# Second cross-attention of a two-layer decoder: scores one slot earlier, two row buffers, copies dealt out in turn

## The chip, the cores and the metric

The kernel runs on one core of a Trainium2 chip. The metric is the device time of one execution in microseconds. Five engines work side by side, each on its own in-order list of instructions, and wait for each other through counting semaphores: TensorE (PE; its weight loads are shown as PEld), VectorE (DVE), ScalarE (ACT), GpSimd (POOL) and SyncE (SP), which here only issues transfers.

## The reference

Two decoder layers over x of shape (8 batches, 256 rows, 256 features), each layer with a mixing step, a cross-attention to a context of the same shape, and a feed-forward step, each followed by residual and layer norm. The change lies in the second layer's cross-attention, 16 heads of 16 features:

```python
def _mha(key, value, query, mask, Wk, bk, Wq, bq, Wv, bv, Wo, bo):
    k, q, v = (heads(a @ W.T + b) for a, W, b in ...)      # (8, 16, 256, 16)
    scores = jnp.einsum('bhmd,bhnd->bhmn', q, k)
    scores = jnp.where(mask, scores, jnp.float32(-10000000000.0))
    attn = jax.nn.softmax(scores / jnp.sqrt(jnp.float32(DK)), axis=3)
    out = jnp.einsum('bhmn,bhnv->bhmv', attn, v)
    out = out.transpose(0, 2, 1, 3).reshape(bs, n_q, EDIM)
    return out @ Wo.T + bo
x = _layernorm(x + _L1_xattn_ref(ctx_1024, ctx_1024, x, mask, ...))
```

(the first line stands for the three projections of the reference.) The layer norm follows in the same stage, and the gated feed-forward step after it.

## The kernel before, in words

The stage is `attention_mask`, with one function per engine: `mask_pe`, `mask_act`, `mask_dve`, `mask_pool`, `mask_sp`. Every engine's list is written out by hand; nothing is reordered. Work goes in 32 rounds n = 4b + j (batch b = 0..7, j = 0..3), four heads g = 0..3 a round. For round n:

- **scores(n)** on PE (16 matmuls, L1553 in batch 0, L1556 in the others) fills four PSUM banks, one per head g. It waits until all peaks of round n-1 have read them.
- **peaks(n, g)** on DVE (L1877, two instructions a head) adds the mask bias, writes the rows to SBUF (`Sx` for g 0 and 1, `Pr` for g 2 and 3) and takes the row maximum into `mq`.
- **exps(n, g)** on ACT (L1779, two instructions a head) applies exp to the rows in place.
- **turn(n, g)** on PE (L1572, four transposes) turns the rows into one of two PSUM banks, `t_bank[g % 2]`. Heads 0 and 2 share one bank, 1 and 3 the other, so turn(n, 2) waits until head 0 has been copied out, and turn(n, 3) until head 1 has.
- **turned(n, g)** copies the bank to SBUF: DVE for g 0 and 1 (L1885), ACT for g 2 and 3 (L1787).
- **weigh(n)** on PE (16 matmuls, L1587) multiplies with the values; **copy_ot(n)** on ACT (L1796) keeps the result. weigh(n-1) is issued at the end of round n.

Because there is one set of row buffers and one `mq`, peaks(n+1, g) waits for turn(n, g). The first cross-attention of the kernel (lines 701 to 1047) does the same arithmetic with two row buffers and another order of its lists.

Once a batch, one bank `m_bank` carries in turn: the query projection of a later batch (`x1_project_q`, L242), two turnings back of the attention output (`turn_back`, L1596) with DVE's division by the row sums (`normalise`, L1895 and L1901), the transposes of it (L234) with ACT's copy (`turn_at`, L1807), the output projection (`project_rows`, L250) with DVE's residual sum and moments (`norm_begin`, parts 0, 1, 2, L201 to L216), and the transposes of the finished rows (L234) with ACT's copy (`turn_x`, L1801). POOL builds the mask bias, splits queries and keys into two parts, and finishes the layer norm; SP loads values and masks and moves the split parts between partitions.

Before the change round n on PE is: turn 0, turn 1, scores(n+1), turn 2, turn 3, then weigh(n-1); the work on `m_bank` lies between these, mostly ahead of weigh. After the 32nd round begins the gated feed-forward step: `gate_up`, `tanh`, `hidden` and so on, whose first parts are already mixed into the last round.

Of the kernel before, what the change touches and what calls it, by code (L numbers as in the profile page):

```python
# [27 lines left out]
P = 128  # L28
# [68 lines left out]
def decoder_kernel(nc, xT, ctxT, fside, mask0, mask1, wmats, cols_d, rows_d, gb, gate_up, down,  # L97
                   ident_d, rel_k_d, rel_v_d, mix_d, consts_d, out):
    ctx = ExitStack()
    with ctx:  # L100
# [1354 lines left out]
        def attention_mask(sa_y_mm, sa_y_steps, sa_biased, sa_kept, sa_xt_mm, sa_xt_sb, sa_r_out):  # L1455
# [55 lines left out]
            def down_bank(t, tt):  # L1511

                if t < B - 2:
# [8 lines left out]
            rows_of = [Sx[:, :, :, :].rearrange("p a t k -> p (a t) k"),  # L1522
                       Pr[:, :, :, :].rearrange("p a t k -> p (a t) k")]
# [11 lines left out]
            def rows_of(g, t):  # L1535

                return (Sx if g < 2 else Pr)[:, g % 2, t, 0:S]
# [23 lines left out]
            def mask_pe(pe):  # L1561

                def turn(n, g):

                    pe.wait_ge(p_exp, 4 * n + g + 1)
                    if g < 2:
                        ge(pe, pt_act, 2 * (n - 1) + g + 1)
                    else:
                        pe.wait_ge(pt_dve, 2 * n + g - 1)
                    for t in range(TT):  # L1570
                        for k in range(TT):
                            last = pe.transpose(t_bank[g % 2][:, k * S + t * P:k * S + (t + 1) * P],  # L1572
                                                rows_of(g, t)[:, k * P:(k + 1) * P], ident[:, :])
                    last.then_inc(t_mm, 1)
# [74 lines left out]

                def second_round(b, n):  # L1650

                    turn(n, 0)
                    if b >= 2:
                        pe.wait_ge(y_steps, 4 * (b - 2) + 1)
                    if b >= 3:
                        pe.wait_ge(kept, b - 2)
                        transpose_tiles(pe, m_bank, x_tok[:, b - 3, :, :], xt_mm)
                    turn(n, 1)
                    scores(pe, n + 1)
# [6 lines left out]
                    if b >= 1:  # L1666
                        if b >= 3:
                            pe.wait_ge(xt_sb, b - 2)
                        if b == 1:
                            pe.wait_ge(q_sb, 3)  # L1670
                        pe.wait_ge(ot_sb, NQ * b)
                        turn_back(b - 1, 0)
                    weigh(n - 1)

                def third_round(b, n):

                    turn(n, 0)
                    if b >= 1:
                        pe.wait_ge(normed, TT * (b - 1) + 1)
                        turn_back(b - 1, 1)  # L1680
                    turn(n, 1)
                    scores(pe, n + 1)
                    if b >= 1:
                        pe.wait_ge(normed, TT * b)
                        transpose_tiles(pe, m_bank, at, at_mm)
                    turn(n, 2)
                    turn(n, 3)
                    if b < B - 2:
                        if b >= 1:
                            pe.wait_ge(at_sb, b)  # L1690
                        else:
                            pe.wait_ge(sa_xt_sb, B)
                        x1_project_q(pe, b + 2, m_bank)
                    weigh(n - 1)
# [4 lines left out]
                def fourth_round(b, n):  # L1699

                    turn(n, 0)
                    turn(n, 1)
                    if b < B - 1:
                        scores(pe, n + 1)
                    else:
# [3 lines left out]
                    if 1 <= b < B - 1:  # L1709
                        pe.wait_ge(at_sb, b)  # L1710
                        if b < B - 2:
                            pe.wait_ge(q_sb, b + 3)
                        project_rows(pe, m_bank, aT, wo, y_mm)
# [59 lines left out]
            def mask_act(act):  # L1773

                def exps(n, g):

                    for t in range(TT):
                        act.wait_ge(s_max, TT * (4 * n + g) + t + 1)
                        last = act.activation(rows_of(g, t), rows_of(g, t), ACT.Exp,  # L1779
                                              bias=mq[:, g, t:t + 1], scale=-1.0)  # L1780
# [28 lines left out]

                for b in range(B):  # L1810
                    for j in range(NQ):
                        n = NQ * b + j
                        if n >= 1:
                            turned(n - 1, 2)
                        exps(n, 0)
                        exps(n, 1)
                        if n == 0:
                            x1_copy_q(act, 1, o_bank)
# [4 lines left out]
                        if j == 3 and b < B - 2:  # L1823
                            x1_copy_q(act, b + 2, m_bank)
                        if n >= 1:
                            turned(n - 1, 3)
                        exps(n, 2)
                        exps(n, 3)
                        if j == 1 and b >= 3:
                            turn_x(b - 3)  # L1830
                        if n >= 2:
                            copy_ot(n - 2)
                        if j == 2 and b >= 1:
                            turn_at(b - 1)

# [13 lines left out]
                turned(NQ * B - 1, 2)  # L1849
                turned(NQ * B - 1, 3)  # L1850
# [15 lines left out]
            def mask_dve(dve):  # L1866

                def peaks(n, g):
# [6 lines left out]
                    ge(dve, t_mm, 4 * (n - 1) + g + 1)  # L1875
                    for t in range(TT):
                        dve.tensor_tensor_reduce(  # L1877
                            out=rows_of(g, t), in0=s_bank[g][:, t * S:(t + 1) * S],
                            in1=x1_bias_two[:, b % 2, t, :], scale=-1.0, scalar=3e38, op0=ALU.add,
                            op1=ALU.min, accum_out=mq[:, g, t:t + 1]).then_inc(s_max, 1)  # L1880
# [25 lines left out]

                for b in range(B):
                    for j in range(NQ):
                        n = NQ * b + j
                        peaks(n, 0)  # L1910
                        peaks(n, 1)
                        if j == 2 and b >= 1:
                            normalise(b - 1, 0)
                        peaks(n, 2)
                        peaks(n, 3)
# [1456 lines left out]
```

## Time and profile before

| what | value |
|---|---|
| median of 3 runs | 820.91 us (820.75 to 822.95) |
| the profiled execution's own time | 820.36 us |
| its span in the trace | 818.6 us |
| PE busy | 778.7 us, 95% |
| DVE busy | 646.8 us, 79% |
| ACT busy | 615.9 us, 75% |
| POOL busy | 429.8 us, 53% |
| mean granted TensorE clock | 0.998 of full speed |

The 1.8 us between the execution's time and the span lie outside the trace. Busy time is shown per engine; a busy PE can still run its blocks with gaps between them that its pipelined records cover, so block starts say more than busy time. The stage of the change goes from about 561 us to about 737 us of the span.

### The profile page before, as it was taken

How to read it: one execution, taken by the hardware profiler on the slowest of the kernel's cores; microseconds unless marked ns; L12 is line 12 of the kernel's file. 1: busy time of each engine (PE TensorE's matmuls, PEld its weight loads, DVE VectorE, ACT ScalarE, POOL GpSimd, SP SyncE). 2: the span in 40 equal slices, each digit the busy share in tenths (PEclk: the TensorE clock that was granted, in tenths of full speed). 3: DMA queues.
4: the chain of work that ended last, by engine and by line, in shares of the span. 5: the costliest groups of instructions: out<-in, count | busy, mean ns of one | idle time of the engine just before them, and what ended most of it. 6: DMA issues, size and time to landing. Idle time of an engine off the chain costs nothing.

```text
span 818.6 us, 20952 instructions
## 1 busy us (share of the span) xinstructions
PE 778.7 (95%) x6901; PEld 596.0 (73%) x6901; DVE 646.8 (79%) x2457; ACT 615.9 (75%) x1602; POOL 429.8 (53%) x462
## 2 busy tenths in 40 slices
PE   9998999999999988999999999999899999999996
PEld 7876777777667766677777777777577777676785
DVE  4997888888998866778778667775888888976776
ACT  4547998888993467888887888875999999984331
POOL 0265475676755165354553644126855666335764
PEclk9999999999999999999999999999999999999999
DMA  9400663222203378988988989864121222200001
GB/s 316 153 26 35 199 188 68 79 85 86 73 15 132 127 219 278 293 256 255 283 240 255 272 242 275 268 184 158 50 65 67 68 70 69 66 2 0 27 26 53
DMA packets 105393, 115.05 MB, mean 141 GB/s; under 512 B 29061, under 2 KB 94085, under 8 KB 105030
## 3 DMA queue, kind: packets, MB, share of 16 engines
q1 hardware_dynamic: 104724, 113.35, 44.4%
q8 instruction: 57, 0.93, 0.5%
q14 instruction: 50, 0.41, 0.2%
q10 hardware_dynamic: 562, 0.35, 0.1%
HBM read 48.09 MB, written 51.82 MB: 122 GB/s over the span
## 4 chain that ended last, share of the span: by engine, by line
PE 49%; ACT 7%; DVE 5%; issue 2%; DMA 2%; POOL 1%; SPq 0%; DVEq 0%; ACTq 0%
PE bank L1572 7%; PE bank L242 6%; PE bank L2336 6%; PE bank L250 5%; PE bank L2322 3%; PE bank L2353 3%; PE bank L1587 3%; PE bank L1623 3%; PE bank L1613 3%; PE bank L1556 2%; PE bank L2388 2%; ACT Sx L1779 2%; PE bank L2370 1%; PE bank L234 1%; ACT q_heads L1787 1%
## 5 line engine op out<-in xcount | busy, mean ns | idle before, releaser
L242 PE MATMUL bank<-x_feat,w_all_mats 128*128 128x256 f32 x384 | 93.0, 386 | 1.9 <-ACT q_full L358 0.6
L242 PEld LDWEIGHTS bank<-x_feat,w_all_mats 128*128 128x128 f32 x384 | 70.4, 191 | 14.7 <-ACT rw L2711 3.8
L2669 ACT ACTIVATE bias_area<-bias_area,mq_two 128x256 f32<-128x256 f32 x128 | 66.5, 533 | 0.0
L3065 POOL TENSOR_TENSOR bnd<-bnd,consts 128x60 f32<-128x60 f32 x64 | 18.6, 312 | 81.3 <-DMA bnd<-band_scratch 81.2
L3054 POOL COPY rw<-rw 128x856 f32<-128x856 f32 x32 | 29.2, 913 | 57.9 <-ACT rw L2711 57.9
L894 ACT ACTIVATE dist<-dist,mq_two 128x256 f32<-128x256 f32 x128 | 56.0, 501 | 3.6 <-DVE mq_two L1008 3.6
L2845 DVE COPY q_heads<-bank 128x512 f32<-128x512 f32 x64 | 41.7, 685 | 21.0 <-PE bank L2336 21.0
L1779 ACT ACTIVATE Sx<-Sx,mq 128x256 f32<-128x256 f32 x128 | 54.3, 501 | 2.3 <-DVE mq L1877 2.3
L1885 DVE COPY q_heads<-bank 128x512 f32<-128x512 f32 x64 | 42.0, 684 | 17.0 <-PE bank L1572 17.0
L1008 DVE CUSTOM_DVE_ANT_0 dist<-bank,bias_area 128x256 f32<-128x256 f32 x128 | 46.5, 419 | 10.7 <-PE bank L701 5.6
L1779 ACT ACTIVATE Pr<-Pr,mq 128x256 f32<-128x256 f32 x128 | 54.5, 505 | 0.0
L1877 DVE CUSTOM_DVE_ANT_0 Sx<-bank,bias_area 128x256 f32<-128x256 f32 x128 | 46.5, 419 | 1.6 <-PE bank L1553 1.2
L2837 DVE CUSTOM_DVE_ANT_0 bias_area<-bank,dist 128x256 f32<-128x256 f32 x128 | 46.1, 420 | 1.2 <-DMA dist<-skew_scratch 1.2
L1877 DVE CUSTOM_DVE_ANT_0 Pr<-bank,bias_area 128x256 f32<-128x256 f32 x128 | 46.5, 420 | 0.0
L1787 ACT ACTIVATE q_heads<-bank 128x512 f32<-128x512 f32 x64 | 37.7, 591 | 11.5 <-PE bank L1572 11.5
L250 PE MATMUL bank<-w_all_mats,aT 128*128 128x256 f32 x192 | 46.3, 384 | 0.0
L1016 DVE COPY q_heads<-bank 128x512 f32<-128x512 f32 x64 | 43.9, 686 | 2.1 <-PE bank L713 1.9
L902 ACT ACTIVATE q_heads<-bank 128x512 f32<-128x512 f32 x64 | 38.0, 593 | 10.0 <-PE bank L713 8.9
L1572 PE MATMUL bank<-ident,Sx 128*128 128x128 f32 x256 | 38.9, 282 | 5.5 <-ACT q_heads L1787 5.1
L1572 PEld LDWEIGHTS bank<-ident,Sx 128*128 128x128 f32 x256 | 27.3, 141 | 22.1 <-issue 10.3
L2678 ACT ACTIVATE q_heads<-bank 128x512 f32<-128x512 f32 x64 | 37.8, 592 | 4.5 <-PE bank L2336 4.5
L2336 PE MATMUL bank<-ident,bias_area 128*128 128x128 f32 x256 | 39.8, 290 | 0.7 <-DVE q_heads L2845 0.6
(322 smaller groups left out, 2377.5 us busy)
## 6 DMA issues: line engine op xcount, KB each, us to landing
dist<-skew_scratch SPq DMA_DIRECT2D x64, 296.0 KB, 4.1
skew_scratch<-rw SPq DMA_DIRECT2D x30, 588.0 KB, 5.3
bnd<-band_scratch SPq DMA_DIRECT2D x64, 108.0 KB, 2.9
band_scratch<-bias_area SPq DMA_DIRECT2D x32, 162.0 KB, 3.2
band_scratch<-bias_area SPq DMA_DIRECT2D x32, 148.0 KB, 2.6
skew_scratch<-dist SPq DMA_DIRECT2D x4, 1024.0 KB, 9.1
context_values<-dist SPq DMA_DIRECT2D x8, 512.0 KB, 2.6
v_two<-context_values SPq DMA_DIRECT2D x8, 512.0 KB, 4.2
```

The lines of the kernel that those rows point to most:

```text
L242: last = pe.matmul(dst[:, m * S:(m + 1) * S], w[:, k, m * P:(m + 1) * P], rhs[:, k, :], start=(k == 0), stop=(k == FT - 1))
L250: last = pe.matmul(dst[:, t * D:(t + 1) * D], src[:, k, t * P:(t + 1) * P], w[:, k, :], start=(k == 0), stop=(k == FT - 1))
L894: last = act.activation(rows_of(n, g, t), rows_of(n, g, t), ACT.Exp, bias=mq_two[:, n % 2, g, t:t + 1], scale=-1.0)
L1008: dve.tensor_tensor_reduce(out=rows_of(n, g, t), in0=s_bank[g][:, t * S:(t + 1) * S], in1=bias_two[:, b % 2, t, :], scale=-1.0, scalar=3e3 ...
L1016: dve.tensor_copy(PTq[:, 4 * (n % 2) + g, :, :], t_bank[g % 2][:, :].rearrange("p (k q) -> p k q", k=TT))\
L1572: last = pe.transpose(t_bank[g % 2][:, k * S + t * P:k * S + (t + 1) * P], rows_of(g, t)[:, k * P:(k + 1) * P], ident[:, :])
L1779: last = act.activation(rows_of(g, t), rows_of(g, t), ACT.Exp, bias=mq[:, g, t:t + 1], scale=-1.0)
L1787: act.activation(PTq[:, 4 * (n % 2) + g, :, :], t_bank[g % 2][:, :].rearrange("p (k q) -> p k q", k=TT), ACT.Copy).then_inc(pt_act, 1)
L1877: dve.tensor_tensor_reduce(out=rows_of(g, t), in0=s_bank[g][:, t * S:(t + 1) * S], in1=x1_bias_two[:, b % 2, t, :], scale=-1.0, scalar=3e3 ...
L2336: last = pe.transpose(t_bank[g % 2][:, k * S + t * P:k * S + (t + 1) * P], rows_of(n, g)[:, t, k * P:(k + 1) * P], ident[:, :])
L2669: last = act.activation(rows_of(n, g)[:, t, :], rows_of(n, g)[:, t, :], ACT.Exp, bias=mq_two[:, n % 2, g, t:t + 1], scale=-1.0, accum_out= ...
L2837: dve.tensor_tensor_reduce(out=rows_of(n, g)[:, t, :], in0=s_bank[g][:, t * S:(t + 1) * S], in1=dist_pairs[:, t, 2 * j + g // 2, :, g % 2] ...
```

## The change

The rows of odd rounds get a second place (the last quarter or so of `dist`, and `bnd`), and the row maxima go to the two halves of `mq_two`, so that peaks(n, g) waits for turn(n-2, g) instead of turn(n-1, g). On PE scores(n+1) moves to the front of round n, straight behind weigh(n-2). Copies are dealt out by t_bank: DVE copies heads 0 and 2, ACT heads 1 and 3. DVE's and ACT's loops handle peaks and exps of round n+1 together with the copies of round n. A projection or turning stands in the middle of the round, between turn 1 and turn 3, and a second one may stand ahead of weigh. The output projection of a batch moves one round later for the middle batches.

```diff
+            flat = dist[:, :, :, :].rearrange("p t h s -> p (t h s)")
+            rows_odd = [flat[:, (TT * H - 6 + i) * S:(TT * H - 5 + i) * S] for i in range(6)] \
+                + [bnd[:, 0, i * S:(i + 1) * S] for i in range(2)]
-            def rows_of(g, t):
-                return (Sx if g < 2 else Pr)[:, g % 2, t, 0:S]
+            def rows_of(n, g, t):
+                return rows_odd[TT * g + t] if n % 2 else (Sx if g < 2 else Pr)[:, g % 2, t, 0:S]
 # PE
                 def turn(n, g):
                     pe.wait_ge(p_exp, 4 * n + g + 1)
-                    if g < 2:
-                        ge(pe, pt_act, 2 * (n - 1) + g + 1)
-                    else:
-                        pe.wait_ge(pt_dve, 2 * n + g - 1)
+                    ge(pe, (pt_dve, pt_act)[g % 2], 2 * n + g // 2)
                 def first_round(b, n):
+                    scores(pe, n + 1)
                     turn(n, 0)
                     turn(n, 1)
-                    scores(pe, n + 1)
+                    if b >= 2:
+                        pe.wait_ge(at_sb, b - 1)
+                        if b < B - 1:
+                            pe.wait_ge(q_sb, b + 2)
+                        project_rows(pe, m_bank, aT, wo, y_mm)
                     turn(n, 2)
                     turn(n, 3)
...
+                    if b >= 3:
+                        pe.wait_ge(y_steps, 4 * (b - 2) + 1)
+                        pe.wait_ge(kept, b - 2)
+                        transpose_tiles(pe, m_bank, x_tok[:, b - 3, :, :], xt_mm)
                     if b >= 1:
                         weigh(n - 1)
                 def second_round(b, n):
+                    scores(pe, n + 1)
                     turn(n, 0)
                     turn(n, 1)
+                    if b >= 1:
...
+                        turn_back(b - 1, 0)
                     turn(n, 2)
                     turn(n, 3)
...
+                    if b == B - 1:
                         pe.wait_ge(normed, TT * (b - 1) + 1)
                         turn_back(b - 1, 1)
+                    weigh(n - 1)
                 def third_round(b, n):
                     scores(pe, n + 1)
+                    if b == B - 1:
                         pe.wait_ge(normed, TT * b)
                         transpose_tiles(pe, m_bank, at, at_mm)
+                    turn(n, 0)
+                    turn(n, 1)
+                    if 1 <= b < B - 1:
+                        pe.wait_ge(normed, TT * (b - 1) + 1)
+                        turn_back(b - 1, 1)
                     turn(n, 2)
                     turn(n, 3)
+                    if b == 0:
+                        pe.wait_ge(sa_xt_sb, B)
                         x1_project_q(pe, b + 2, m_bank)
                     if b == B - 1:
                         pe.wait_ge(at_sb, b)
                         project_rows(pe, m_bank, aT, wo, y_mm)
+                    weigh(n - 1)
                 def fourth_round(b, n):
+                    if b < B - 1:
+                        scores(pe, n + 1)
                     turn(n, 0)
                     turn(n, 1)
+                    if 1 <= b < B - 1:
+                        pe.wait_ge(normed, TT * b)
+                        transpose_tiles(pe, m_bank, at, at_mm)
+                    if b == B - 1:
                         gate_up(0)
                     turn(n, 2)
                     turn(n, 3)
+                    if 1 <= b < B - 2:
                         pe.wait_ge(at_sb, b)
+                        x1_project_q(pe, b + 2, m_bank)
                     weigh(n - 1)
 # ACT, inside the loop over b and j (exps(0, 0..3) and x1_copy_q(1) stand ahead of it)
+                        if j == 3 and b == 0:
+                            x1_copy_q(act, 2, m_bank)
+                        if j == 0 and 2 <= b < B - 1:
+                            x1_copy_q(act, b + 1, m_bank)
+                        if n >= 2:
+                            copy_ot(n - 2)
...
                         if j == 1 and b >= 3:
                             turn_x(b - 3)
+                        if j == 2 and b == B - 1:
                             turn_at(b - 1)
+                        if more:
+                            exps(n + 1, 0)
+                        turned(n, 1)
+                        if j == 3 and 1 <= b < B - 1:
+                            turn_at(b - 1)
+                        if more:
+                            exps(n + 1, 1)
+                        turned(n, 3)
+                        if more:
+                            exps(n + 1, 2)
+                            exps(n + 1, 3)
 # DVE, inside its loop (peaks(0, 0..3) and a norm_begin stand ahead of it)
+                        if more:
+                            peaks(n + 1, 0)
+                        turned(n, 0)
+                        if j == 1 and b == B - 1:
                             normalise(b - 1, 0)
...
+                        if more:
+                            peaks(n + 1, 1)
+                            peaks(n + 1, 2)
                         if j == 0 and b >= 2:
...
                             norm_begin(dve, y_steps, b - 2, y_mm, b - 1, m_bank, True, parts=(0,))
+                        if more:
+                            peaks(n + 1, 3)
+                        turned(n, 2)
+                        if j == 0 and b >= 2:
+                            norm_begin(dve, y_steps, b - 2, y_mm, b - 1, m_bank, True, parts=(1, 2))
                         if n == 0:
                             keep_late(dve, KV_LATE)
+                        if j == 1 and 1 <= b < B - 1:
+                            normalise(b - 1, 0)
+                        if j == 1 and b == B - 1 or j == 2 and 1 <= b < B - 1:
                             normalise(b - 1, 1)
```

## Rows read from the trace of the kernel before

**Rows 1.** Windows: busy us (instructions) of PE, PEld, DVE, ACT, POOL, clock, DMA

```profile
156.26:179.67 23.41, 23.10 (x240) 17.99 (x236) 21.01 (x91) 21.02 (x52) 17.12 (x16) 1.00 0.21 75
566.08:586.66 20.58, 19.48 (x197) 14.01 (x195) 17.42 (x75) 18.39 (x45) 15.76 (x14) 1.00 0.13 43
586.66:608.79 22.13, 20.62 (x225) 14.80 (x222) 19.36 (x86) 21.25 (x53) 15.05 (x11) 1.00 0.20 63
...
651.34:672.61 21.27, 20.94 (x225) 15.11 (x226) 18.96 (x84) 19.83 (x49) 13.99 (x13) 1.00 0.20 67
...
693.88:714.21 20.33, 19.30 (x218) 13.72 (x218) 18.97 (x84) 19.00 (x47) 8.53 (x9) 1.00 0.21 67
714.21:729.95 15.74, 15.42 (x169) 11.16 (x170) 14.23 (x65) 14.61 (x36) 4.55 (x5) 1.00 0.01 2
729.95:818.60 88.65, 77.57 (x465) 64.78 (x463) 59.99 (x133) 32.57 (x60) 51.17 (x47) 0.98 0.07 25
```

**Rows 2.** Waits in 651.34 to 672.61 us: total us, times, longest

```profile
DVE q_heads L1885 <- PE bank L1572: 2.2, 2, 1.4
```

**Rows 3.** Timeline of PE, first cross-attention: start, us, engine, line, operation

```profile
156.26 0.74 PE L701 MATMUL bank<-x_k_even,x_q_cells 32*128 32x256 f32 x16
...
157.87 1.89 PE L250 MATMUL bank<-w_all_mats,aT 128*128 128x256 f32 x8
159.59 1.04 PE L713 MATMUL bank<-ident,Pr 128*128 128x128 f32 x8
160.56 1.07 PE L728 MATMUL bank<-q_heads,v_two 128*32 128x256 f32 x16
161.56 0.75 PE L701 MATMUL bank<-x_k_even,x_q_cells 32*128 32x256 f32 x16
```

**Rows 4.** Timelines of PE, ACT and DVE, first cross-attention, its fourth round

```profile
86.06 0.75 PE L701 MATMUL bank<-x_k_odd,x_q_cells 32*128 32x256 f32 x16
...
88.48 0.63 PE L713 MATMUL bank<-ident,Pr 128*128 128x128 f32 x4 [0.65 <-DVE q_heads L1016]
89.78 0.63 PE L713 MATMUL bank<-ident,Pr 128*128 128x128 f32 x4 [0.68 <-ACT q_heads L902]
...
91.34 0.75 PE L701 MATMUL bank<-x_k_odd,x_q_cells 32*128 32x256 f32 x16
...
88.24 0.91 ACT L894 ACTIVATE dist<-dist,mq_two 128x256 f32<-128x256 f32 x2
89.04 0.60 ACT L902 ACTIVATE q_heads<-bank 128x512 f32<-128x512 f32 x1
...
86.96 0.42 DVE L1008 CUSTOM_DVE_ANT_0 dist<-bank,bias_area 128x256 f32<-128x256 f32 x1 [1.33 <-issue]
...
87.65 0.69 DVE L1016 COPY q_heads<-bank 128x512 f32<-128x512 f32 x1
88.25 0.41 DVE L1008 CUSTOM_DVE_ANT_0 dist<-bank,bias_area 128x256 f32<-128x256 f32 x1
```

**Rows 5.** Timelines of PE, DVE and ACT, 561 to 569 us

```profile
561.45 1.15 PE L1553 MATMUL bank<-c_feat,q_par 32*128 32x256 f32 x16
...
562.80 0.42 DVE L1877 CUSTOM_DVE_ANT_0 Sx<-bank,bias_area 128x256 f32<-128x256 f32 x1 [0.79 <-PE bank L1553]
...
563.26 1.71 ACT L1779 ACTIVATE Sx<-Sx,mq 128x256 f32<-128x256 f32 x4 [2.33 <-DVE mq L1877]
...
567.01 1.70 ACT L1779 ACTIVATE Pr<-Pr,mq 128x256 f32<-128x256 f32 x4
```

**Rows 6.** Timeline of DVE: moments of one batch; one division

```profile
566.28 0.76 DVE L207 BATCH_NORM_STATS2 st<-y_sb 128x6 f32<-128x256 f32 x2
...
567.50 1.28 DVE L1885 COPY q_heads<-bank 128x512 f32<-128x512 f32 x2
...
661.57 0.25 DVE L1895 RECIPROCAL rl<-bank 128x16 f32<-128x16 f32 x1
...
662.27 1.28 DVE L1885 COPY q_heads<-bank 128x512 f32<-128x512 f32 x2
```

More of the change, by code:

```diff
@@ L1650, in second_round @@
                 def second_round(b, n):
+                    scores(pe, n + 1)
                     turn(n, 0)
[L1653 to L1657, printed above, removed]
-                    turn(n, 1)
-                    scores(pe, n + 1)
+                    turn(n, 1)
+                    if b >= 1:
+                        if b >= 3:
+                            pe.wait_ge(xt_sb, b - 2)
+                        elif b == 2:
+                            pe.wait_ge(y_steps, 1)
+                        else:
+                            pe.wait_ge(q_sb, 3)
+                        pe.wait_ge(ot_sb, NQ * b)
+                        turn_back(b - 1, 0)
                     turn(n, 2)
@@ L1778, in exps @@
                         act.wait_ge(s_max, TT * (4 * n + g) + t + 1)
[L1779 to L1780 removed]
+                        last = act.activation(rows_of(n, g, t), rows_of(n, g, t), ACT.Exp,
+                                              bias=mq_two[:, n % 2, g, t:t + 1], scale=-1.0)
                     last.then_inc(p_exp, 1)
@@ L1808, in turn_at @@
                                    ACT.Copy).then_inc(at_sb, 1)
+                exps(0, 0)
+                exps(0, 1)
+                x1_copy_q(act, 1, o_bank)
+                exps(0, 2)
+                exps(0, 3)
                 for b in range(B):
@@ L1812, in mask_act @@
                         n = NQ * b + j
[L1813 to L1818, printed above, removed]
+                        more = n + 1 < NQ * B
+                        if j == 3 and b == 0:
[4 more added lines that the diff above has]
+                            copy_ot(n - 2)
                         if n == 2:
@@ L1905, in normalise @@
                     last.then_inc(normed, 1)
+                for g in range(4):
+                    peaks(0, g)
+                dve.wait_ge(sa_biased, B)
+                dve.wait_ge(sa_kept, B - 1)
+                norm_begin(dve, sa_y_steps, B - 1, sa_y_mm, B, m_bank, True)
                 for b in range(B):
@@ L1909, in mask_dve @@
                         n = NQ * b + j
-                        peaks(n, 0)
-                        peaks(n, 1)
-                        if j == 2 and b >= 1:
-                            normalise(b - 1, 0)
-                        peaks(n, 2)
-                        peaks(n, 3)
+                        more = n + 1 < NQ * B
+                        if more:
+                            peaks(n + 1, 0)
+                        turned(n, 0)
+                        if j == 1 and b == B - 1:
+                            normalise(b - 1, 0)
+                        if j == 3 and b == B - 1:
+                            dve.wait_ge(biased, b)
+                            dve.wait_ge(kept, b - 1)
+                            norm_begin(dve, y_steps, b - 1, y_mm, b, m_bank, True, parts=(0,))
+                        if more:
+                            peaks(n + 1, 1)
+                            peaks(n + 1, 2)
                         if j == 0 and b >= 2:
```

66 lines of the change are left out of this document (8 added, 58 removed).

## The prediction

> **What bounds the kernel now.** I read the windows first, cut at the starts of batches in the second cross-attention [rows 1]. A steady batch takes 21.27 us (651.34 to 672.61). In it PE is busy 20.94, ACT 19.83, DVE 18.96 and POOL 13.99 us, and TensorE has its full clock, 2.4 GHz. So three engines are nearly full at once. The reader should see that none can be relieved alone, and that the records of neighbouring instructions overlap, so busy time overstates the work. The view of waits for the same batch names DVE's wait for PE's transposes as its largest, 2.2 us [rows 2]: DVE has slack that the order of the lists takes from it.
>
> The best witness is in the same trace: the first cross-attention already has two row buffers, scores in front of the round and copies split by bank. Its PE blocks give pitches [rows 3]: from scores to the work in mid-round (scores and eight transposes) 1.61 us, a projection 1.72, eight transposes 0.97 (four: 0.49), weigh 1.00. It has four projections a batch, one in the middle of each round, and takes 23.41 us [rows 1]. By these pitches its PE work is about four times (1.61 + 0.97 + 1.00) = 14.32, four projections 6.88, and three groups of four transposes 1.47: 22.7. PE is 97% packed there. The changed stage has two projections and four such groups: 14.32 + 3.44 + 1.96 = 19.7 us of PE work against 21.27 now. That 1.5 us a batch is all that a better order can win.
>
> **What the change does to a steady batch.** Nothing is removed or added in the loop: 16 score matmuls, 16 transposes, 16 weighing matmuls, eight peaks, eight exps and four copies a round stay, as do the transfers. The row places only change addresses. What changes is who waits for whom, so I walk the new lists.
>
> In a round that has no projection in the middle a short loop closes: scores fill the banks, DVE takes peak 0 and only then copies head 0 out of the transpose bank that turn 2 needs; ACT does exps 0 and only then copies head 1, which turn 3 needs. The first cross-attention has just one such round, its fourth [rows 4]. Scores start at 86.06, peak 0 at 86.96, the copy 0.69 later, turn 2 0.83 after the copy's start; ACT's exps start at 88.24, its copy 0.80 later, turn 3 0.74 after that, at 89.78. PE idles 0.65 and 0.68 us, and the next scores come at 91.34: 5.28 us for 3.58 us of work. There ACT was late with earlier work. When it isn't, exps start 0.46 after the peak (562.80 to 563.26) [rows 5]. From peak 0 to turn 3 is then 0.46 + 0.80 + 0.74 = 2.00 us, and by way of DVE's copy and turn 2, 0.69 + 0.83 + 0.49 = 2.01: the same. Turn 3 then lasts 0.56 (89.78 to 91.34 less weigh) and weigh 1.00, so peak 0 to next scores is 3.56. From scores to peak 0 I take 0.80 us: 0.90 in rows 4 is the upper bound and the end of the scores block (0.75) the lower. A plain round is 4.36 us. ACT's own work is close to that (its 19.83 us a batch over four rounds, less overlaps), so I take 4.5.
>
> DVE's list sets when peak 0 can come. With DVE busy throughout, peak 0 to the next peak 0 is four heads of 0.69, two copies of 0.60 and one division of 0.70 [rows 4, 6]: 4.66 us. Batch b from 3 to 5, with t = 0 at its first scores:
> - j = 0: peak 0 at 0.80; three heads and a copy to 3.47; the residual sum waits for the projection, 1.61 + 1.72 plus about 0.3, so 3.65, and takes about what a copy of the same size does, 4.25; last head 4.94; copy 5.54; moments 1.22 (566.28 to 567.50) [rows 6]: 6.76. PE gets through its projection and transposes by 5.8 and is not what is late.
> - j = 1: peak 0 at 6.76. j = 2: 6.76 + 4.66 = 11.42. j = 3: 16.08. PE is ahead of DVE at each.
> - After j = 3's peak 0: 3.56, and the query projection now stands ahead of weigh, 1.72. Next batch at 21.36.
>
> So a steady batch costs 21.36 us against 21.27: nothing is won, because the 1.5 us of PE gaps come back as waits at turn 2 and turn 3 in the three rounds whose middle holds only 0.49 us of transposes. This is the step on which the forecast stands. The bounds: from peak 0 of j = 0 to that of j = 3, 15.28 us, DVE works without a pause but for 0.2, so shorter latencies only help in the rest; with each of its steps (to peak, to exps, to turn) 0.1 us shorter the batch takes 21.0, with rows 4's lateness of ACT (88.24 instead of 87.42, 0.8 us) in one round 22.2.
>
> **The ends of the stage.** Each is set against its window [rows 1].
> - Batch 0, from 566.08: the exps of heads 2 and 3 start at 567.01 behind the query copy and take 1.6 [rows 5]; exps of the next round at 568.61, turn 3 at 570.15, context product and next scores at 572.43. The scores of this batch are slower, 561.45 to the peak at 562.80, 1.35 [rows 5]; I take 1.3. Rounds 1 to 3: 1.3 + 3.56 + 0.49, 1.3 + 3.56 + 1.72, and 4.36. End 588.7 against 586.66: +2.1.
> - Batch 1: 4.5 + 4.5, then DVE at 4.66 twice, with the projection last: about 20.0 against 22.13: -2.1, of which 1.72 is only the output projection moved out to batch 2.
> - Batches 2 to 5: +0.1 each: +0.4. Batch 6: no query projection, 19.64 against 20.33: -0.7.
> - Batch 7, up to the 32nd round: it now holds two output projections (+1.72). In j = 2 its transposes stand ahead of turn 0 and wait for both divisions: peaks and copies end at 11.4, second division 12.1, transposes 12.3 to 12.8, ACT's copy from 13.0, exps 13.4, turn 3 at 15.0, then 0.56 + 1.72 + 1.00: 18.3 against 15.74: +2.5.
> Sum: 2.1 - 2.1 + 0.4 - 0.7 + 2.5 = +2.2 us. From the 32nd round on (88.65 us) the order on PE is the same, the gate product standing in mid-round in both, and `tanh` waits for PE's transposes behind weigh, so the delay is passed on whole. Of the 820.36 us of the profiled execution that makes 822.6; the median is 0.55 above that execution, so 823.1.
>
> **Moved work that hides.** The query copy of a batch comes at the head of the next batch, about a round later. POOL's split and four to six transfers on SP's queue behind it must land before the scores at j = 3, about 15 us on. All POOL work of a batch is 13.99 us [rows 1], and this is less than half of it, so I cost it at nothing; if the transfers were late, PE would wait at j = 3's scores, and everything behind. The new waits of peaks (for turns two rounds back) are long over. ACT and DVE alternate copies and rows more often. Here a row and a rule differ: peak 0 starts at 86.96 and, two instructions of 0.42 later, the copy at 87.65, so an instruction occupies 0.345 of its 0.42 us and a change of kind costs nothing [rows 4]. The Trainium skill, VectorE: DVE Perf Modes, section "The DRAIN you can't avoid", says that after each operation there is a flush of its duration less 266 ns, sooner only if the next is not held. Taken literally that would make it an estimated 0.57 us an instruction, and both kernels alike far slower than the trace shows; the measured pitch decides.
>
> **Rivals.**
> - Faster, at the packing of the first cross-attention: PE work 19.7 plus its 0.7 us of loss a batch is 20.4, 0.9 less than now. Over batches 2 to 6 that is -4.5, and with ends no better than I have them about -3: 818, at best 816. For it: the same structure packs PE to 97% there. Against it: there every round has 1.72 us in the middle to cover the loop of 2.8 us from scores to turn 3; here three of four have 0.49, and DVE alone needs the 15.28 us above. The point that decides is whether turn 3 of such rounds waits. The Trainium skill, Perfetto Trace Analysis, section "Optimization Strategies", asks for the matrix engine to be kept as busy as possible by speeding up the engines that block it, and by that this rival would win; the fourth round of rows 4 shows the blocking instead.
> - Slower, ACT's backlog: if ACT stays late as at 88.24, the round costs 0.8 more each time a query or feature copy stands ahead of exps 0, once in each of batches 2 to 6 and twice in the ends: +5.6 on the forecast, 828.7. Against it: in j = 0 ACT idles about 0.8 us waiting for turn 3 behind the projection, which drains it.
> - No change at all (within 1 us): the 32nd round's start is not passed on whole, because DVE copies one head and not two there; at most 0.6 less, or latencies slightly shorter: 821.
>
> **How the numbers follow.** Forecast (+1 to +4.5 us) 0.60, centre 823.0. Faster rival 0.16, no change 0.13, backlog or late transfers 0.11. A measurement tells 0.3%, 2.5 us, from no change. Of the forecast case a little more than half lies above +2.5: slower 0.33 + 0.11 = 0.44; same 0.27 + 0.13 + 0.02 of the faster rival's weak end = 0.42; faster 0.14. The range reaches from 817.0, inside the faster rival, to 827.0. The forecast case alone spans 822 to 825.5.
>
> **What would show it.** In the trace after: three rounds of each batch with PE waiting at turn 2 or 3 for DVE's or ACT's copy, 0.3 to 0.6 us each, and none in j = 0; batches of 21.0 to 21.7 us; DVE without idle time from j = 0 to j = 3 and idle about 2 us after it; the 32nd round at about 732. I am wrong if batches take 20.5 us (latencies smaller or the loop hidden), or if scores wait for transfers.

## The result, and the profile after

| | before | after |
|---|---|---|
| median | 820.83 us (820.73 to 822.95, 4 runs) | 829.61 us (828.37 to 831.39, 4 runs) |
| profiled execution, its span | 820.36, 818.6 | 828.9, 827.1 |
| first scores of the stage to first gate product | 169.29 (561.45 to 730.74) | 178.56 (560.72 to 739.28) |
| gate product to the end of the span | 87.86 | 87.82 |

The ratio is 1.0108 [1.0091, 1.0125]: the change makes the kernel 8.8 us slower. The forecast was 823.0 with a range up to 827.0, so it missed. The third line of the table is the better ruler: the stage is 9.27 us longer, and what follows it is unchanged, as the fourth shows. I call it the stage's length below.

Windows of the kernel after, cut where PE begins the first round of each batch, which it now does with the scores of the next round (columns as in [rows 1], with which the rows compare from batch 1 on):

```profile
565.45:587.86 22.41, 19.46 (x199) 14.01 (x198) 17.72 (x80) 20.30 (x49) 16.02 (x14) 1.00 0.12 40
587.86:608.92 21.06, 18.96 (x217) 13.34 (x214) 17.87 (x79) 20.02 (x50) 9.29 (x7) 1.00 0.21 67
608.92:631.49 22.57, 20.16 (x225) 14.85 (x222) 19.37 (x84) 19.58 (x48) 12.11 (x10) 1.00 0.18 62
631.49:654.07 22.58, 20.67 (x229) 15.27 (x225) 19.38 (x84) 20.07 (x49) 13.96 (x12) 1.00 0.20 63
...
699.22:720.03 20.81, 18.92 (x220) 13.84 (x216) 18.97 (x84) 18.31 (x45) 13.95 (x12) 1.00 0.20 65
720.03:738.43 18.40, 16.90 (x180) 12.60 (x176) 15.63 (x67) 16.34 (x40) 4.54 (x5) 1.00 0.00 1
```

A steady batch takes 22.58 us; the forecast had 21.36 and before took 21.27. PE's own busy time in it is not larger than before (20.67 against 20.94), so the 1.3 us are waiting. In the kernel after `turn` is L1570, `turn_back` L1594, `exps` L1784, `copy_ot` L1801, and the copies of turned rows are L1792 on ACT and L1898 on DVE; in later runs some of these numbers are a few higher. The view of waits for 640 to 662 us, after:

```profile
PEld bank L1570 <- ACT dist L1784: 1.1, 1, 1.1
...
ACT w_all_mats L1801 <- PE bank L1594: 1.0, 1, 1.0
...
PE bank L1570 <- ACT q_heads L1792: 0.9, 1, 0.9
PE bank L1570 <- DVE q_heads L1898: 0.8, 2, 0.4
```

In the same view of the kernel before (651.34 to 672.61 us) `copy_ot` has no wait, PE has none for DVE's copies, and its wait for ACT's copy is short:

```profile
PE bank L1572 <- ACT q_heads L1787: 0.3, 1, 0.3
```

The third round of the batch, from the timelines of PE and of ACT, after:

```profile
642.10 0.75 PE L1557 MATMUL bank<-x_k_cells,x_q_cells 32*128 32x256 f32 x16
642.77 1.09 PE L1570 MATMUL bank<-ident,Sx 128*128 128x128 f32 x8
643.70 0.60 PE L1594 MATMUL bank<-ident,w_all_mats 128*128 128x128 f32 x4
644.70 0.63 PE L1570 MATMUL bank<-ident,Pr 128*128 128x128 f32 x4 [0.40 <-DVE q_heads L1898]
646.20 0.63 PE L1570 MATMUL bank<-ident,Pr 128*128 128x128 f32 x4 [0.88 <-ACT q_heads L1792]
...
647.76 0.51 PE L1557 MATMUL bank<-x_k_cells,x_q_cells 32*128 32x256 f32 x8
```

```profile
641.70 1.70 ACT L1784 ACTIVATE Pr<-Pr,mq_two 128x256 f32<-128x256 f32 x4
644.40 0.38 ACT L1801 ACTIVATE w_all_mats<-bank 128x256 f32<-128x256 f32 x1 [1.01 <-PE bank L1594]
644.68 0.89 ACT L1784 ACTIVATE dist<-dist,mq_two 128x256 f32<-128x256 f32 x2
645.48 0.58 ACT L1792 ACTIVATE q_heads<-bank 128x512 f32<-128x512 f32 x1
```

The reader should read the two together. ACT is free after its exps, at 643.4, and then waits 1.01 us with `copy_ot(n-2)` at the head of its list. That copy is the first of batch b to write `OTq`, so it waits until PE has turned the old contents back, and the change has put `turn_back(b-1, 1)` (643.70) into the middle of this very round. Behind the copy stand exps 0 and the copy of head 1, for which PE's fourth turning waits 0.88 us. PE waits for ACT, which waited for PE.

### The profile page after: what moved, and what is told of

It reads as the page before. It is cut to its first block, busy times and chain, and to the rows that moved or that the text cites. A ratio compares the mean times of both kernels' runs of the same rounds, so it can differ in the third digit from the quotient of the medians.

```text
span 827.1 us, 20951 instructions
## 1 busy us (share of the span) xinstructions
PE 777.5 (94%) x6901; PEld 596.8 (72%) x6901; DVE 648.5 (78%) x2457; ACT 617.5 (75%) x1602; POOL 429.0 (52%) x462
## 4 chain that ended last, share of the span: by engine, by line
PE 43%; DVE 10%; ACT 9%; issue 4%; POOL 1%; DMA 1%; SPq 0%; DVEq 0%; ACTq 0%
PE bank L242 6%; PE bank L2354 6%; PE bank L1570 4%; PE bank L250 4%; PE bank L2340 3%; PE bank L2371 3%; PE bank L1621 3%; PE bank L1611 3%; PE bank L1585 2%; PE bank L2406 2%; ACT dist L1784 2%; DVE q_heads L1898 2%; PE bank L2388 2%; ACT bias_area L2687 1%; PE bank L1557 1%
## 5 line engine op out<-in xcount | busy, mean ns | idle before, releaser
L3083 POOL TENSOR_TENSOR bnd<-bnd,consts 128x60 f32<-128x60 f32 x64 | 18.3, 308 | 79.0 <-DMA bnd<-band_scratch 79.0
L894 ACT ACTIVATE dist<-dist,mq_two 128x256 f32<-128x256 f32 x128 | 56.1, 502 | 3.6 <-DVE mq_two L1008 3.6
L2863 DVE COPY q_heads<-bank 128x512 f32<-128x512 f32 x64 | 41.7, 685 | 20.6 <-PE bank L2354 20.6
L1008 DVE CUSTOM_DVE_ANT_0 dist<-bank,bias_area 128x256 f32<-128x256 f32 x128 | 46.5, 420 | 10.7 <-PE bank L701 5.6
L1898 DVE COPY q_heads<-bank 128x512 f32<-128x512 f32 x64 | 43.8, 685 | 4.1 <-PE bank L1570 4.1
L1016 DVE COPY q_heads<-bank 128x512 f32<-128x512 f32 x64 | 43.9, 686 | 2.0 <-PE bank L713 1.9
L1890 DVE CUSTOM_DVE_ANT_0 dist<-bank,bias_area 128x256 f32<-128x256 f32 x96 | 35.4, 418 | 12.7 <-PE bank L1557 11.6
L1784 ACT ACTIVATE dist<-dist,mq_two 128x256 f32<-128x256 f32 x96 | 43.2, 500 | 2.0 <-DVE mq_two L1890 1.9
L1792 ACT ACTIVATE q_heads<-bank 128x512 f32<-128x512 f32 x64 | 37.7, 589 | 8.0 <-PE bank L1570 7.9
L250 PEld LDWEIGHTS bank<-w_all_mats,aT 128*128 128x128 f32 x192 | 34.7, 190 | 7.1 <-issue 3.2
L2354 PEld LDWEIGHTS bank<-ident,bias_area 128*128 128x128 f32 x256 | 35.1, 207 | 6.2 <-issue 3.6
L2340 PE MATMUL bank<-k_two,q_par 32*128 32x256 f32 x512 | 36.7, 400 | 0.7 <-DVE mq_two L2855 0.5
L2705 ACT ACTIVATE w_all_mats<-bank 108x512 f32<-108x512 f32 x32 | 19.1, 598 | 24.1 <-PE bank L2388 23.6
```

The costliest lines, as they stand in the source:

```text
L250: last = pe.matmul(dst[:, t * D:(t + 1) * D], src[:, k, t * P:(t + 1) * P], w[:, k, :], start=(k == 0), stop=(k == FT - 1))
L894: last = act.activation(rows_of(n, g, t), rows_of(n, g, t), ACT.Exp, bias=mq_two[:, n % 2, g, t:t + 1], scale=-1.0)
L1008: dve.tensor_tensor_reduce(out=rows_of(n, g, t), in0=s_bank[g][:, t * S:(t + 1) * S], in1=bias_two[:, b % 2, t, :], scale=-1.0, scalar=3e3 ...
L1016: dve.tensor_copy(PTq[:, 4 * (n % 2) + g, :, :], t_bank[g % 2][:, :].rearrange("p (k q) -> p k q", k=TT))\
L1784: last = act.activation(rows_of(n, g, t), rows_of(n, g, t), ACT.Exp, bias=mq_two[:, n % 2, g, t:t + 1], scale=-1.0)
L1898: dve.tensor_copy(PTq[:, 4 * (n % 2) + g, :, :], t_bank[g % 2][:, :].rearrange("p (k q) -> p k q", k=TT))\
```

## The experiments

### The missed wait: earlier, later

e1_ot_late, with one copy moved a few places down ACT's list in six of 32 rounds:

```diff
+ot_late = j == 2 and 1 <= b < B - 1
-if n >= 2:
+if n >= 2 and not ot_late:
     copy_ot(n - 2)
 ...
 turned(n, 1)
+if ot_late:
+    copy_ot(n - 2)
```

> The changed kernel, with one step of ScalarE's list moved: at j = 2 of batches 1 to 6 the copy of the weighed output, copy_ot(n - 2), stands behind the first copy of turned rows instead of at the head of the round. Theory A (the copy at the head waits for the second turning back, which the change put in the middle of the same round, and holds exps 0, the copy of head 1 and so turn 3): the wait of 1.01 us of that copy and the 0.88 us of PE at turn 3 in j = 2 go; a batch falls from 22.58 to about 21.4 us, the kernel by 6 to 7 us from 829.6 to about 823. Rival B (the rounds are long because rows go through peak, exps and copy before turn 2 and turn 3, whatever that copy does): the batch stays within 0.3 us of 22.58 and the kernel at 828 to 830.

Measured: 824.77 us (823.66 to 827.54), ratio 1.0054 [1.0038, 1.007]; stage 173.09, 5.47 shorter than after, or 0.91 for each of the six places, a little less than the 6 to 7 us expected. The same stretch of ACT, and the window of the steady batch:

```profile
643.61 0.91 ACT L1784 ACTIVATE dist<-dist,mq_two 128x256 f32<-128x256 f32 x2 [0.25 <-DVE mq_two L1893]
644.42 0.57 ACT L1792 ACTIVATE q_heads<-bank 128x512 f32<-128x512 f32 x1
644.90 0.37 ACT L1801 ACTIVATE w_all_mats<-bank 128x256 f32<-128x256 f32 x1
...
631.46:653.15 21.69, 20.49 (x228) 15.29 (x225) 19.27 (x84) 19.95 (x49) 13.97 (x12) 1.00 0.20 66
```

Exps 0 start 1.55 us after the round's scores (642.06) where after had 2.58, the wait is gone, and the fourth turning follows the third without a pause.

e2_back_later is the same dependence drawn out: after, with the turning back one place later on PE.

```diff
 turn(n, 1)
+turn(n, 2)
 if 1 <= b < B - 1:
     pe.wait_ge(normed, TT * (b - 1) + 1)
     turn_back(b - 1, 1)
-turn(n, 2)
 turn(n, 3)
```

> The changed kernel, with one step of PE's list moved the other way: in the third round of batches 1 to 6 the second turning back stands behind turn 2 instead of ahead of it. PE's own work is the same. Theory A: ScalarE's copy at the head of the round waits about 1.5 us longer (2.5 instead of 1.01), turn 3 comes as much later, and the kernel rises by about 6 x 1.4 = 8 us to about 838. Rival B: turn 2 no longer waits behind the turning, the round keeps its length, 829 to 830.

Measured: 843.12 us (842.32 to 847.11), ratio 1.0288 [1.0263, 1.0313]; stage 191.02, 12.46 us longer than after. The way through ACT's list grows, because the turning back now stands behind a turning that itself waits for DVE (ACT, then PE):

```profile
651.66 0.39 ACT L1801 ACTIVATE w_all_mats<-bank 128x256 f32<-128x256 f32 x1 [2.47 <-PE bank L1594]
...
650.50 0.63 PE L1570 MATMUL bank<-ident,Pr 128*128 128x128 f32 x4 [0.83 <-DVE q_heads L1898]
650.96 0.60 PE L1594 MATMUL bank<-ident,w_all_mats 128*128 128x128 f32 x4
653.47 0.63 PE L1570 MATMUL bank<-ident,Pr 128*128 128x128 f32 x4 [1.91 <-ACT q_heads L1792]
```

The 12.46 us have two parts. A batch in which nothing else happens takes 24.04 us for 22.58, which is 1.46 more, exactly what the copy's wait grew by; six times this is 8.8 us, the size that was expected. The other 3.7 us lie in batches 1, 4 and 5, which are 1.2, 1.0 and 1.5 us longer still: there TensorE's granted clock fell. Windows of batches 3 and 4, and of 2 us in batch 1:

```profile
637.29:661.33 24.04, 20.69 (x229) 15.28 (x225) 19.37 (x84) 20.08 (x49) 13.95 (x12) 1.00 0.19 59
661.33:686.41 25.08, 21.93 (x229) 16.69 (x225) 19.46 (x84) 20.35 (x49) 13.95 (x12) 0.93 0.18 57
...
605.00:607.00 2.00, 2.00 (x21) 0.70 (x20) 0.00 (x0) 1.86 (x5) 0.00 (x0) 0.50 0.00 0
```

Steady batches go 21.69, 22.58, 24.04 us while the wait of the copy goes 0, 1.01, 2.47. The missed wait is thereby shown from both sides.

### The second set of row buffers

e3_one_set takes it away from the kernel after; e4_sets_alone gives it to the kernel before.

```diff
 # e3_one_set: after, rows and waits of one set
-return rows_odd[TT * g + t] if n % 2 else (Sx if g < 2 else Pr)[:, g % 2, t, 0:S]
+return (Sx if g < 2 else Pr)[:, g % 2, t, 0:S]
 ...
-if n >= 2:
-    dve.wait_ge(t_mm, 4 * (n - 2) + g + 1)
+ge(dve, t_mm, 4 * (n - 1) + g + 1)
 # e4_sets_alone: before, with the opposite edit and mq_two
```

> The changed kernel with one set of row buffers again: peaks(n, g) waits for turn(n - 1, g), and everything else of the change stays. Theory A says nothing of it. If the second set is what makes the new order possible, peaks 2 and 3 of the next round wait behind turn 2 and turn 3 of this one; with turn 3 at about 2.8 us after the scores and peak 3 due 2.7 us after them, the cost is 0.3 to 1 us in each of 31 rounds: 838 to 860. If the set buys nothing, 829 to 831.

> The kernel before with nothing of the change but the second set of row buffers and of maxima: peaks(n, g) waits for turn(n - 2, g). In the old order peaks of round n + 1 come behind the scores that are issued after turn 1, so only the peaks of heads 2 and 3 could start sooner, and they stand 1.4 us behind the first in the list. Expected by the walk of the prediction: no wait of the kernel before is for this, 820 to 821.5. Rival: the set itself costs, by its place in dist and bnd (slower instructions or transfers), some 0.5% or more: 825.

Measured: e3_one_set 846.06 us (845.14 to 846.41), ratio 1.0309 [1.0295, 1.0323]; e4_sets_alone 820.5 us (819.1 to 822.37), ratio 1.0001 [0.9991, 1.0011], its stage 169.28 against 169.29. So the sets alone do nothing in the old order, and the new order needs them: without them it would be 16 us worse again. In e3_one_set's waits (637.88 to 662.56 us) peaks (L1889) wait for turnings, and pass that on to exps and later turnings:

```profile
DVE Sx L1889 <- PE bank L1570: 3.7, 4, 2.5
...
PE bank L1570 <- DVE q_heads L1897: 2.4, 3, 0.8
ACT Sx L1784 <- DVE mq_two L1889: 2.4, 3, 1.1
```

What the change costs lies in its lists, not in its buffers.

### What covers the small loop

e5_q_mid starts from e1_ot_late and exchanges the two pieces of `m_bank` work in the fourth round of batches 1 to 5, the 1.72 us projection going to the middle:

```diff
 # PE, j == 3
 turn(n, 1)
-transpose_tiles(pe, m_bank, at, at_mm)
+x1_project_q(pe, b + 2, m_bank)
 turn(n, 2)
 turn(n, 3)
-pe.wait_ge(at_sb, b)
-x1_project_q(pe, b + 2, m_bank)
+pe.wait_ge(q_sb, b + 3)
+transpose_tiles(pe, m_bank, at, at_mm)
 # ACT, j == 3: x1_copy_q behind exps 1, turn_at behind exps 2
```

> e1_ot_late (824.8 us) with one more move in batches 1 to 5: in the fourth round the query projection (1.72 us) stands in the middle, and the transposes of the normalised output (about 0.5) stand at the end ahead of weighing, with ScalarE's two copies moved to follow them. Theory (the loop turning, copy back, turning is only hidden where something of more than its 0.4 stands between the two pairs of turnings, and a projection hides it whole): in e1 the fourth round has both pieces and still shows a wait of 0.40 ahead of its third turning; with the projection in the middle that wait goes and the batch shortens by about 0.4 to 0.55, from 21.69 to about 21.2, so some 2 to 2.7 us over five batches: 822 to 823. Rival (VectorE's and ScalarE's work sets the batch, not the loop): the order of PE's pieces inside the round makes no difference, 824.5 to 825.5.

Measured: 821.6 us (820.37 to 823.26), ratio 1.0001 [0.9986, 1.0016]; stage 170.27, 2.82 below e1_ot_late. A steady batch is 21.13 us for 21.69. Only half of that is cover. The fourth round, where the two pieces were exchanged, is 0.30 us shorter in each of batches 1 to 5 (6.15 for 6.45), 1.5 us in all. The other 1.3 us come in the second round of batches 2 to 6, 0.26 us each (4.37 for 4.63 in a steady batch), where PE's order is the same in both kernels. There VectorE's moments, which stand ahead of peak 0, last 1.25 us from the first of them to the next peak, and 1.52 in e1_ot_late:

```profile
656.22 0.74 DVE L207 BATCH_NORM_STATS2 st<-y_sb 128x6 f32<-128x256 f32 x2
...
657.35 0.17 DVE L216 TENSOR_SCALAR ve<-mv 128x2 f32<-128x2 f32 x1
657.47 0.42 DVE L1899 CUSTOM_DVE_ANT_0 Sx<-bank,bias_area 128x256 f32<-128x256 f32 x1
```

So the expected 0.4 to 0.55 us a batch was met by luck: the loop gave 0.30, and what the moments gave was not foreseen (the last section comes back to it). In the batch's first round, which has a projection in the middle too, PE's timeline has no wait at all:

```profile
650.69 0.75 PE L1557 MATMUL bank<-x_k_cells,x_q_cells 32*128 32x256 f32 x16
651.37 1.09 PE L1570 MATMUL bank<-ident,Sx 128*128 128x128 f32 x8
652.30 1.89 PE L250 MATMUL bank<-w_all_mats,aT 128*128 128x256 f32 x8
654.03 1.04 PE L1570 MATMUL bank<-ident,Pr 128*128 128x128 f32 x8
655.07 0.66 PE L234 MATMUL bank<-ident,x_tok 128*128 128x128 f32 x4
655.66 1.07 PE L1585 MATMUL bank<-q_heads,v_two 128*32 128x256 f32 x16
656.66 0.39 PE L1557 MATMUL bank<-x_k_cells,x_q_cells 32*128 32x256 f32 x4
```

That round takes 5.97 us of nothing but PE blocks. The change's other loss, 0.30 us in each of five batches, is told by the fourth round: the change put four transposes (0.5 us) where cover was needed, and the projection where none was.

### VectorE's moments, moved into its idle time

```diff
-if j == 0 and b >= 2:
+if b >= 2 and j == (0 if b == B - 1 else 3):
     norm_begin(dve, y_steps, b - 2, y_mm, b - 1, m_bank, True, parts=(1, 2))
```

> e5_q_mid with the moments and the normalising of a finished tile (two of three parts, about 1 us of VectorE) moved from the first round of a batch to its fourth in batches 2 to 6, where VectorE stood idle for about 2 us. Theory (VectorE runs without a pause from the first round of a batch to its fourth, so what is taken out of that stretch shortens the batch as long as PE's 20.5 us of work isn't met): batch about 20.8, so 819.5 to 821. Rival (ScalarE's chain of exponentials sets the pace, or PE's own work): no gain over e5_q_mid within 0.5 us.

Measured: 826.36 us (825.52 to 834.55), ratio 1.0065 [1.0041, 1.0088]; stage 175.40. Both theories miss: it is 5.1 us longer than e5_q_mid. PE's timeline says why:

```profile
666.20 0.74 PE L1557 MATMUL bank<-x_k_cells,x_q_cells 32*128 32x256 f32 x16 [1.61 <-DMA x_k_cells<-x_k_cells]
```

The scores wait 1.61 us for the next batch's keys. POOL waits for the moments with the statistics of the finished tile at the head of its list, and behind them stands the splitting of queries and keys, whose transfers the scores need. From POOL's timeline, its wait for the moments (the instruction `rstd<-ve`) and the keys' second half in e6_q_mid_moments, then the same two in e5_q_mid:

```profile
649.82 0.73 POOL L2113 TENSOR_TENSOR rstd<-ve,neghalf 128x2 f32<-128x2 f32 x1 [8.75 <-DVE ve L216]
...
659.79 2.39 POOL L2099 TENSOR_TENSOR x_k_cells<-c_feat,x_k_cells 128x1024 fp32r<-128x1024 f32 x1
```

```profile
652.57 2.37 POOL L2099 TENSOR_TENSOR x_k_cells<-c_feat,x_k_cells 128x1024 fp32r<-128x1024 f32 x1
...
657.60 0.72 POOL L2113 TENSOR_TENSOR rstd<-ve,neghalf 128x2 f32<-128x2 f32 x1 [0.75 <-DVE ve L216]
```

The keys' half starts 10.2 us after its batch's first scores (649.55) in the first, 1.9 us after them (650.69) in the second. It happens in three batches, 4 to 6; in the last batch PE waits 1.50 us more, ahead of the transposes of the finished rows. Of the batches not struck, batch 2 gains 0.7 (608.00 to 628.44, in e5_q_mid 608.43 to 629.56), but batch 3, the first full one, takes 21.11 us against 21.13. In e5_q_mid peak 0 of such a batch's second round already comes 0.81 us after the scores (656.66, 657.47) with the moments ahead of it, and 0.79 us pass even where VectorE waits for nothing but the scores (650.69, 651.48). So VectorE no longer sets the pace there, and its relief is worth nothing. In batch 2, whose first round is 0.66 us shorter for want of finished rows to turn (5.31 and 5.97 us), it still did.

### The two ends of the stage

e7_all adds to e6_q_mid_moments an edit in the last batch; e8_start adds to e5_q_mid one in batch 0, and e9_both_ends has e8_start and the last batch's edit:

```diff
 # last batch, third round (e7_all, e9_both_ends); turn_at moves with it on ACT
-transpose_tiles(pe, m_bank, at, at_mm)
 turn(n, 0)
 turn(n, 1)
+transpose_tiles(pe, m_bank, at, at_mm)
 # batch 0, rounds 0, 1 and 2 (e8_start, e9_both_ends)
 turn(n, 1)
+project_context(pe, KV_LATE)      # in the others: transpose_tiles, x1_project_q
 turn(n, 2)
 turn(n, 3)
-project_context(pe, KV_LATE)
```

> e6_q_mid_moments, and in the last batch's third round the transposes of the normalised output stand between the second and third turning and not ahead of the first, where in e1 PE waited 0.55 us for VectorE's division and 0.26 for the scores' bank. Theory: these 0.5 to 0.8 us go, and the small loop is hidden there too: 0.5 to 0.9 below e6_q_mid_moments. Rival: the divisions' wait moves to the projection at the round's end, which needs the copy of these transposes: no difference.

> e5_q_mid (821.6 us) with, in batch 0, the late keys' projection (1.82), the transposes of the previous stage's last tile (0.5) and the query projection (1.8) moved from behind the fourth turning of their rounds to between the second and third. In e5 these three rounds show waits of 0.68, 0.48, 0.57 and 0.57 us ahead of a third or fourth turning while their piece stands at the round's end. Theory (what the order costs in batch 0 is the uncovered loop turning, copy back, turning): 1.5 to 2.0 us of these go, 819.6 to 820.1. Rival (batch 0 is held by VectorE's and ScalarE's filling, with no work in hand yet): under 0.5 us, 821.2 or more.

> e8_start with, in the last batch's third round, the transposes of the normalised output put between the second and third turning and not ahead of the first (in e5 PE waited 0.54 for VectorE's division there, and 0.44 ahead of its third turning). Theory: 0.5 to 0.9 below e8_start, so about 819.0 to 819.5, and below the kernel before. Rival: the wait moves to the projection at the round's end, which needs the copy of these transposes: no difference from e8_start.

| kernel | median us | ratio to before | stage us |
|---|---|---|---|
| e7_all | 825.95 | 1.0058 [1.0035, 1.008] | 174.65 |
| e8_start | 819.81 | 0.9999 [0.9983, 1.0016] | 169.04 |
| e9_both_ends | 818.82 | 0.9987 [0.9969, 1.0005] | 168.10 |

The last batch's edit is worth 0.75 us on e6_q_mid_moments and 0.94 on e8_start, about as expected. Batch 0's gives 1.23 in the stage, less than the 1.5 to 2.0 expected, because part comes back one round later. In e5_q_mid the fourth round of batch 0 waited 0.65 once and took 4.46 us (584.27 to 588.73); in e9_both_ends it takes 5.27, with both turnings late:

```profile
580.99 0.74 PE L1557 MATMUL bank<-x_k_cells,x_q_cells 32*128 32x256 f32 x16
...
583.40 0.63 PE L1570 MATMUL bank<-ident,dist 128*128 128x128 f32 x4 [0.65 <-DVE q_heads L1905]
584.70 0.63 PE L1570 MATMUL bank<-ident,bnd 128*128 128x128 f32 x4 [0.67 <-ACT q_heads L1795]
...
586.26 0.75 PE L1557 MATMUL bank<-x_k_cells,x_q_cells 32*128 32x256 f32 x16
```

e9_both_ends has the shortest stage of all, 1.2 us under the kernel before and 10.5 under the one after. In whole executions its interval still touches 1, so it beats the kernel after but is not shown to beat the one before.

## Why the prediction was wrong

The step that failed is in the walk of a steady batch: "When it isn't, exps start 0.46 after the peak", and from it peak 0 to next scores 3.56 us in every round after j = 0. It took ACT to be free whenever the rows were ready. In j = 2 it isn't: `copy_ot` waits at the head of ACT's round for a block that the change moves into that round. I had listed the copies' and exps' order but not what each copy waits for, and of the new waits I named only those of peaks. Measured: exps 0 start 1.03 us later in the round than in e1_ot_late, which costs 0.91 us of stage on average in batches 1 to 6, 5.47 us in all. The prediction named two signs of being wrong, batches of 20.5 us and scores that wait for transfers; neither came, and the failure was of a third kind.

One reading of the trace was wrong too: DVE's 2.2 us of [rows 2] is not the largest wait of that view. Two of POOL's are longer, 4.2 us for DVE's moments and 2.7 us for ACT's query copy. It changes no term of the sum, but the first of these waits is the one that grew to 8.75 us in e6_q_mid_moments.

The other steps, against the 9.2 us by which the 32nd round lies farther from the stage's first scores than before (177.71 and 168.50; forecast +2.2):

- **Steady batch 21.36.** Without the missed wait it is 21.69 (e1_ot_late). Of the 0.33 over, 0.30 is one mis-sized term: the moments, taken as 1.22 us from [rows 6], last 1.52 here (e1_ot_late, first and last of them below, then the next peak). It comes in batches 2 to 6, some 1.5 us in all (the 1.3 us that e5_q_mid won back in second rounds are of this), and with the missed wait it accounts for the 7.0 us by which the sum was short.

```profile
636.99 0.74 DVE L207 BATCH_NORM_STATS2 st<-y_sb 128x6 f32<-128x256 f32 x2
...
638.12 0.48 DVE L216 TENSOR_SCALAR ve<-mv 128x2 f32<-128x2 f32 x1
638.51 0.41 DVE L1893 CUSTOM_DVE_ANT_0 Sx<-bank,bias_area 128x256 f32<-128x256 f32 x1
```

- **VectorE without a pause from j = 0 to j = 3** held in e1_ot_late, 15.54 us from peak 0 to peak 0 (632.25 to 647.79) for 15.28 forecast. **The loop** held too: PE waits 0.40 us at the third turning of each of the last three rounds, 0.3 to 0.6 forecast, none in j = 0.
- **Batch 0** was forecast at 588.7 - 561.45 = 27.25 us from the first scores and took 27.14 (560.72 to 587.86). **Batch 1**: 20.0 forecast, 21.06 after; without the wait 19.99 (589.77 to 609.76 in e1_ot_late). **Batch 7**: 18.3 and 18.40. **Batch 6**: 19.64 and 20.81; without the wait 19.94, and the moments are the rest.
- **The rest passed on whole** held: the fourth line of the table.
- **Moved work that hides.** No scores waited for transfers after the change. e6_q_mid_moments shows how near that was: with one step of VectorE three rounds later, POOL's splitting came 8.3 us later, and they did.
- **Rivals.** The faster one failed at the point that it named: turnings of rounds with 0.5 us in the middle do wait. Even with the projection moved there a steady batch takes 21.13 us, not its 20.4. Its sum was also a microsecond too low: -4.5 and the forecast's own ends, +2.5, make -2, not -3. The slower one, 828.7, came nearest in time and in saying that ACT would be late by about 0.8 us a batch. But it laid this to query and feature copies ahead of exps 0, and they cost nothing here: behind them ACT still waited for DVE's peak 0, 0.37 and 0.17 us in the kernel after, and the first round takes 5.97 us both in e1_ot_late, with the query copy at its head, and in e5_q_mid, without it. The cause was a copy that waits. It had too small a chance, 0.11, because I argued against the causes I knew and not for the absence of others.

What stays open: why the moments last longer in some kernels, why the clock fell in three batches of e2_back_later and not in the other three, and whether an order exists that gives batch 0's 0.8 us back.

## What to carry to other kernels

When a list is reordered by hand, write beside every instruction that stands at the head of a round what it waits for, and look where the other engine's new list puts that. A wait for a block issued in the same round closes a loop between two engines, and a place farther costs not only the block that is passed but what that block waits for (0.60 us moved past 0.63 cost 1.46 a batch here). Put the longest piece that needs no answer between the two uses of a buffer, not behind them. Before moving work into an engine's idle time, follow who waits for its result: a third engine's queue may hold a transfer behind it.

## What the runs showed of the hardware

The code ahead of the stage is the same in all kernels, yet its first scores start anywhere from 560.38 (e9_both_ends) to 563.96 us (e8_start) of the span. In the latter the granted clock was lower for a while, in unchanged code (windows of e8_start):

```profile
260.00:280.00 20.00, 18.52 (x85) 14.90 (x84) 14.81 (x44) 6.14 (x11) 1.76 (x4) 0.86 0.51 197
280.00:300.00 20.00, 18.61 (x102) 13.40 (x102) 13.67 (x41) 9.64 (x21) 7.46 (x7) 0.97 0.33 102
```

So single spans scatter by more than most edits here are worth. The stage's length is steadier: at clock 1.00 it repeats to 0.01 us between the kernel before and e4_sets_alone (169.29 and 169.28), which differ in the second row buffers alone. The stage of e2_back_later is the exception, with a clock of 0.50 (1.2 GHz of 2.4) for a little over 3 us in three places. In batch 1 PE's weighing block took 1.94 us there, and 1.07 at full clock. Each fall came in the last moments of PE's wait of 1.90 or 1.91 us for ACT's copy, or at most 1.5 us after it. The same wait came in batches 2, 3 and 6, and the clock stayed at 1.00, so what decides it is not shown. All four executions of this kernel had a mean clock of 0.989 to 0.991, those of the kernel after 0.995 to 0.999.

VectorE's smallest instruction, `ve<-mv` on 128x2, took 0.17 to 0.23 us in most places and 0.47 to 0.49 in batches 2 to 6 of after, e1_ot_late and e2_back_later. In all these 15 cases POOL's mask bias had started 0.14 to 0.17 us earlier (e1_ot_late, to be read with 638.12 above):

```profile
637.97 1.94 POOL L624 TENSOR_SCALAR bias_area<-mask_b 128x512 f32<-128x512 uint8 x1
```

Where the mask bias had been running for over a microsecond (e3_one_set) or had ended 0.5 us before (e5_q_mid), it took 0.17. No run moved the mask bias alone, so this is a coincidence in time and not a shown cause. In e5_q_mid it came earlier with the query copy: ACT copies a round sooner, POOL splits sooner, and the mask bias stands behind the splitting in POOL's list.
